# Layer norm of a feed-forward block: the two feature halves are added on VectorE, so that mean and variance are one TensorE product each

## What is computed

```python
x = x + o @ wo
h = shift_token(x)
mu = h.mean(-1, keepdims=True)
var = h.var(-1, keepdims=True)
h = (h - mu) / jnp.sqrt(var + 1e-05) * lg + lb
h = h @ w1 + b1
a, g = jnp.split(h, 2, axis=-1)
h = a * jax.nn.gelu(g, approximate=False)
x = x + h @ w2 + b2
```

## Time and profile before

| | |
|---|---|
| time, median of 3 runs | 2325.43 us (2323.35 to 2335.47) |
| profiled execution, its own time | 2311.7 us |
| span of the profiled execution | 2309.9 us |
| instructions | 28766 |
| PE busy | 2076.8 us, 90% of the span |
| DVE busy | 1063.5 us, 46% |
| ACT busy | 883.8 us, 38% |
| POOL busy | 684.8 us, 30% |
| mean granted TensorE clock | 0.964 |

### The profile page before, as it was taken

One profiled execution on the slowest core, in us unless ns is written; L12 is line 12 of the kernel. 1 busy time (PEld: TensorE's weight loads), 2 busy tenths in 40 slices (PEclk: granted clock), 3 DMA queues, 4 the chain that ended last, 5 costly groups with the idle time before them and its releaser, 6 DMA issues.

```text
span 2309.9 us, 28766 instructions
## 1 busy us (share of the span) xinstructions
PE 2076.8 (90%) x8914; PEld 1222.2 (53%) x8963; DVE 1063.5 (46%) x2012; ACT 883.8 (38%) x2175; POOL 684.8 (30%) x664
## 2 busy tenths in 40 slices
PE   4774999994899999998999999999999998999897
PEld 2532666662555555555555555555555555555553
DVE  5553222221554554553545535354555444554541
ACT  0021333331444445353534344344535353544432
POOL 6073000003532342342323416132252432232310
PEclk9976999997899999999999999999999999999999
DMA  8332221212100010100000001000010200000000
GB/s 248 124 126 96 62 59 59 61 57 55 28 10 1 1 28 1 37 19 29 1 1 10 19 28 28 19 11 1 1 28 1 44 12 19 1 0 1 1 13 15
DMA packets 71768, 78.19 MB, mean 34 GB/s; under 512 B 17156, under 2 KB 63704, under 8 KB 71640
## 3 DMA queue, kind: packets, MB, share of 16 engines
q1 hardware_dynamic: 56104, 58.68, 8.1%
q0 software_dynamic: 12672, 17.87, 3.9%
q10 hardware_dynamic: 2864, 0.01, 0.1%
HBM read 48.19 MB, written 28.35 MB: 33 GB/s over the span
## 4 chain that ended last, share of the span: by engine, by line
PE 52%; issue 8%; DVE 7%; ACT 5%; POOL 4%; DMA 1%; ACTq 0%; POOLq 0%; DVEq 0%
PE pj L1343 12%; PE pj L1252 10%; PE pj L1349 6%; PE ob L1303 6%; PE pj L1317 4%; PE sc L1279 4%; PE pt L1290 3%; DVE swapped L1528 3%; PE pj L1260 2%; POOL x1tok L1475 2%; ACT prob L1409 2%; PE sc L1272 1%; PE pj L1330 1%; PE pj L1242 1%; PE pj L1324 1%
## 5 line engine op out<-in xcount | busy, mean ns | idle before, releaser
L1486 POOL TENSOR_TENSOR qksq<-qkraw 128x512 f32<-128x512 f32 x128 | 162.7, 1296 | 871.1 <-ACT qkraw L1384 870.9
L1252 PE MATMUL pj<-wqkv,xT 128*128 128x512 f32 x768 | 348.4, 604 | 10.2 <-issue 10.2
L1343 PE MATMUL pj<-h,w 128*128 128x512 f32 (+1 forms) x704 | 338.6, 606 | 7.6 <-DVE h L1569 5.7
L1409 ACT ACTIVATE prob<-sc,nm 128x256 f32<-128x256 f32 (+1 forms) x512 | 222.0, 445 | 228.2 <-DVE nm L1543 225.9
L1303 PEld LDWEIGHTS ob<-vv,pT 128*128 128x128 f32 x1792 | 226.2, 195 | 77.3 <-issue 63.7
L1528 DVE TENSOR_TENSOR swapped<-qkraw,tabs 128x256 f32<-128x256 f32 x256 | 254.0, 1031 | 0.0
L1303 PE MATMUL ob<-vv,pT 128*128 128x64 f32 x1792 | 229.0, 275 | 23.7 <-DVE pT L1173 23.7
L1252 PEld LDWEIGHTS pj<-wqkv,xT 128*128 128x128 f32 x768 | 144.0, 193 | 191.5 <-issue 191.1
L1492 POOL TENSOR_TENSOR direct<-direct,swapped 128x512 f32<-128x512 f32 x128 | 187.5, 1480 | 73.3 <-DVE swapped L1528 73.3
L1523 DVE TENSOR_TENSOR direct<-qkraw,tabs 128x512 f32<-128x512 f32 x128 | 102.9, 804 | 203.1 <-ACT qkraw L1384 203.1
L1343 PEld LDWEIGHTS pj<-h,w 128*128 128x128 f32 (+1 forms) x704 | 120.9, 188 | 123.0 <-issue 115.4
(11 more groups left out here) (246 smaller groups left out, 2645.9 us busy)
## 6 DMA issues: line engine op xcount, KB each, us to landing
xt<-slots_x SPq DMA_DIRECT2D x72, 128.5 KB, 2.1
slots_y<-yt SPq DMA_DIRECT2D x72, 128.0 KB, 1.7
xin<-in_x_dram SPq DMA_DIRECT2D x8, 512.0 KB, 4.8
w1m<-in_L_ffn_w_dram SPq DMA_DIRECT2D x8, 512.0 KB, 10.5
w2m<-in_L_ffn_w_dram SPq DMA_DIRECT2D x8, 512.0 KB, 9.9
x1tok<-in_x_dram SPq DMA_DIRECT2D x8, 512.0 KB, 4.8
x_after_moe<-x1tok SPq DMA_DIRECT2D x8, 512.0 KB, 2.6
x1out<-x_after_moe SPq DMA_DIRECT2D x8, 512.0 KB, 4.5
```

Of the source, the lines that this page charges most:

```text
L1252: mm = pe.matmul(o[:, :], xs(s, c, w * P, P), wqkv[:, l, c, k * INNER:(k + 1) * INNER], start=(c == 0), stop=(c == DC - 1))
L1343: mm = pe.matmul(o[0:P if j == NJ - 1 else HJ[j], :], cols, h[:, c, :], start=(c == 0), stop=(c == DC - 1))
L1409: ins = a.activation(prob[:, g % 4, hh, 0:n], sc[par][:, hh, 0:n], ACT.Exp, bias=nm[:, g % 4, hh:hh + 1], accum_out=rs[:, st["win"] % 2, h ...
L1486: pool.tensor_tensor(qksq[:, k * INNER:(k + 1) * INNER], src, src, ALU.mult).then_inc(squared, 1)
```

## The change

Ahead of the mean product, DVE adds the two (shifted) halves of `xT` into `xsq[:, 0, :]`; PE then does one product over that sum instead of two over the halves. After the squares, DVE adds the two halves of `xsq` in place, and PE again does one product instead of two. Two semaphores, `xsum_ready` and `var_in`, hand the sums to PE. DVE's first addition is issued at the end of the step `wo` with c = 1, behind a wait for its own two additions into `xT`; the second is issued in the step `var`, where DVE had nothing before, behind a wait for ACT's squares.

```diff
                         elif kind == "mean":
-                            wait_taken(pe, st["wo_use"], i)
+                            pe.wait_ge(xsum_ready, at(st["ffn"], i, FFN, 1, 1))
                             o = bank(u, i)
-                            for c in range(DC):
-                                mm = pe.matmul(o[:, :], mean_w[:, :], xs(s, c), start=(c == 0), stop=(c == DC - 1))
-                            mm.then_inc(proj_full, 1)
+                            pe.matmul(o[:, :], mean_w[:, :], xsq[:, 0, :], start=True, stop=True).then_inc(proj_full, 1)
                         elif kind == "var":
-                            pe.wait_ge(xsq_ready, at(st["ffn"], i, FFN, 1, 1))
+                            pe.wait_ge(var_in, at(st["ffn"], i, FFN, 1, 1))
                             o = bank(u, i)
-                            for c in range(DC):
-                                mm = pe.matmul(o[:, :], mean_w[:, :], xsq[:, c, :], start=(c == 0), stop=(c == DC - 1))
-                            mm.then_inc(proj_full, 1)
+                            pe.matmul(o[:, :], mean_w[:, :], xsq[:, 0, :], start=True, stop=True).then_inc(proj_full, 1)
...
                             v.tensor_tensor(x_, o[:, :], x_, ALU.add).then_inc(proj_taken[u % NP], 1)
+                            if st["c"] == DC - 1:
+                                wait_taken(v, u - 1, i)
+                                wait_taken(v, u, i)
+                                v.tensor_tensor(xsq[:, 0, :], xs(s, 0), xs(s, 1), ALU.add).then_inc(xsum_ready, 1)
...
+                        elif kind == "var":
+                            v.wait_ge(xsq_ready, at(st["ffn"], i, FFN, 1, 1))
+                            v.tensor_tensor(xsq[:, 0, :], xsq[:, 0, :], xsq[:, 1, :], ALU.add).then_inc(var_in, 1)
```

More of the change, by code:

```diff
@@ L1127, in build @@
             xsq_ready = sem("xsq_ready")
+            xsum_ready = sem("xsum_ready")
+            var_in = sem("var_in")
             rstd_ready = sem("rstd_ready")
```

## The result

The changed kernel took 2358.12 us at the median of 4 runs (2355.45 to 2362.09), the kernel before 2324.39 us beside it. The ratio is 1.0146, 95% interval 1.0108 to 1.0183: slower by 1.5%, where no difference was forecast. In a second session it was 1.0107 (1.0075 to 1.0139). (A session is a set of runs made together on one chip; the kernel before was run in each.)

What follows compares the result with a forecast made beforehand. PE was taken to bound the kernel, with new links nearly cancelling 27.5 us of removed products: -2.5 - 2.4 + 3.1 + 0.4 = -1.4 us, plus 3 for the clock, from 2325.4 to 2327 us, range 2319 to 2334.

Steps and rivals of the forecast that it cites:

- The list and what bounds the kernel: PE, busy 90% of the span, bounds the kernel; 32 products of 0.86 us go, 32 DVE additions come.
- about 28 us less PE busy time: Sign expected in the profile after, from removing two products per layer norm, 27.5 us of PE work.
- Patterns A and B: A: nine layer norms (body blocks one and two, three in the tail), -2.5 us; B: three in block three, -2.4 us.
- The new link: Each DVE addition put ahead of a PE product: 0.68 us plus a 0.04 us hop, 0.72 us.
- patterns A, B and D: The 13 layer norms outside the body's fourth block; D, the tail's third, was put at +0.4 us.
- Pattern C, the first addition: Fourth block of the body, three layer norms: PE's wait for roped covers the addition and the mean's saving, net 0.
- Pattern C, the second addition: Fourth block, variance: the addition stands behind rr and on; 1.90 us standstill less 0.86, +1.04 three times, +3.1 us.
- The clock: Standstills in patterns C and D, four places: a shorter fall of PE's clock at two of them, +3 us.
- The second, the clock: Rival: the longer clock fall at all four late second additions, 13 us, 2337 us, 0.5% slower; chance 0.14.
- The price of the additions: Rival: additions cost 1.56 us each instead of 0.68 in patterns A and B, +21 us, 2347 us; chance 0.06.

Runs made afterwards that it cites:

- e3: The changed kernel with the fourth block of the body (three of 16 layer norms) left in the old form: 1.0017 of the kernel before.
- e5: The changed kernel, but the fourth block's first addition reads one operand from PSUM and skips its wait: 1.0040, again 1.0044, of the kernel before.
- e2: Only the variance product takes its sum from VectorE, the mean stays two products: 2341.47 us, 1.0069 of the kernel before.
- e4: The changed kernel with products of constants on PE ahead of its waits for VectorE's sums: 2330.94 us, 1.0021 of the kernel before.
- e1: Only the mean product takes its sum from VectorE, the variance stays two products: 2347.38 us, 1.0086 of the kernel before.
- e6: The kernel before plus the fourth block's first addition, for which only VectorE's own list waits; PE's products unchanged: 1.0032 of the kernel before.

## Why the prediction was wrong, point by point

**The list and what bounds the kernel: right.** PE bounds it, and of 27.5 us of product time removed none came through. The additions appear where they were forecast, and VectorE's busy time rose by 32.5 us (22 forecast; the 10.5 between are mostly time held). The sign "about 28 us less PE busy time" did not come: it is 8.0 us more.

**Patterns A and B: right in kind.** The new link was priced 0.72 and is 0.80 (0.69 + a hop of 0.10 to 0.11 us). For the 13 layer norms of patterns A, B and D the sum was -4.5 us, -0.2%. The ledger of e3 has -3.4 us for them. In the time nothing of a gain was found: +0.17% (-0.08 to +0.42) in e3 and +0.11% with fillers. So the sum was near, and what it left out, the clock, was as large as the gain.

**Pattern C, the first addition: the first step that failed.** I wrote that the wait for roped "covers a dearer first addition: even at 1.56 us PE comes to the transposes in time", and took 1.56 as the price beside GpSimd, though GpSimd's instructions stand one behind the other here and the earlier trace rows already gave 2.85 as the worst of 128. What came instead: 4.11, 4.12 and 4.78 us of standstill ahead of the mean product in the three rounds, 13.0 us where I had put nothing. With the wait for roped (3.5) that they cover, pattern C is +9.2 us by the ledger and not +3.1.

The rows of before bear a reckoning in place of a price: the addition ends 0.55 us after the GpSimd instructions that it has to wait out. In the row of 1.56 that is one (GpSimd 2175.33 + 1.04 = 2176.37 by the timeline, end 2176.92), in the row of 2.85 two, and in the 4.06 of after the rest of a run of four. How many it is went, in the rows looked at, with how close they stand. Two places of before:

```profile
602.68 2.31 POOL L1486 TENSOR_TENSOR qksq<-qkraw 128x512 f32<-128x512 f32 x2
602.71 2.85 DVE L1523 TENSOR_TENSOR direct<-qkraw,tabs 128x512 f32<-128x512 f32 x1 [1.95 <-ACT qkraw L1384]
...
625.14 2.48 POOL L1486 TENSOR_TENSOR qksq<-qkraw 128x512 f32<-128x512 f32 x2 [4.40 <-ACT qkraw L1384]
625.16 1.56 DVE L1523 TENSOR_TENSOR direct<-qkraw,tabs 128x512 f32<-128x512 f32 x1 [1.95 <-ACT qkraw L1384]
```

At 602 us GpSimd's second instruction began 0.22 us before the first had ended, and VectorE waited out both (end 605.56, GpSimd 604.99). At 625 us it began 0.04 us after the end of the first; there VectorE came in between, 0.54 us after the first, and GpSimd's second took 1.40 us instead of 1.04. In the fourth block the four stand like the first pair, each begun 0.6 us before the end of the one before it. Before the change GpSimd's run at this place ended at 991.47 + 2.63 = 994.10, by the timeline; by that reckoning the mean product, which started at 990.56, would have been put at 994.7, four microseconds late. The Trainium skill (SBUF — State Buffer, section on the two separate sides) says just this: VectorE with two SBUF inputs and a GpSimd instruction that reads SBUF share a pair of ports under an exclusive lock, and the loser waits out the whole instruction. The trace agrees, with e5's 0.68 us for one operand in PSUM beside it, and goes further: VectorE was held not for one instruction but to the end of the run, 4.06 us (three of the four, as it began in the second). I had looked for a price of the addition alone, not for who else was at work at its place.

**Pattern C, the second addition: right.** 1.90 us of standstill were forecast, 1.62 came in each round; e2 has the same 1.62 without the first addition.

**The clock: the second step that failed, and the larger one.** The mechanism was named, its size wrong by far: I put it at 3 us, and at 13 us in the rival with a chance of 0.14. The ledger puts 35.8 - 27.5 = 8.3 us on standstills, 4.8 without the wait for roped; the measured loss is 25 us in one session (1.07% of 2312) and 34 us in the other. So some 20 to 29 us are the clock's, and e4 gives back 20 to 29; by PE's busy time in the profiled execution it is 37. I counted only the four longest new standstills, with a fall at two of them. But 16 layer norms got two each, and those of 0.3 to 3.3 us cost clock too, with no held addition among them: e5 has a clock of 0.955 against 0.961, e3 0.955 against 0.959, and in the changed kernel the tail is at 0.96 against 0.98 before. Not each one does: the block at 785 to 796 us ran at full clock through standstills of 0.74 and 1.88 us. Which do, I can't say from the rows.

**The rivals.** The second, the clock (2337, slower), named the right mechanism and the right way, but tied it to four places and left out the held addition, and 2358 lies far beyond it. The price of the additions as a rival was put everywhere, at 1.56, instead of in one place, at 4 us; and against it I had said that POOL is idle at the places of patterns A and B, which does not hold for the third block, whose three additions took 0.90 us.

**Open.** e1 and e2 add up to 1.55%, the whole change in two sessions 1.46% and 1.07%, with intervals that overlap; whether the sessions differ in it is not settled. The two profiles of the changed kernel say where such a difference would lie: the standstills at the two products are the same (21.9 and 26.0 us, 21.8 and 26.0), while from the first layer norm to the end PE is busy for 1552.1 us in one and 1535.7 in the other, at a clock of 0.96 and 0.97. What sets the clock apart in two executions of one kernel the runs do not show. That no gain was left in the 13 layer norms with fillers is measured, not explained.

## What to carry to other kernels

Before a VectorE instruction with both inputs in SBUF is put on the path, look in the timeline at what GpSimd does at that place: here it was held until GpSimd's whole run of instructions was over, and one operand in PSUM freed it. To take work from a PE that is 90% busy and put a wait in its stead was no gain here, even where the wait was as short as the work: the standstill cost its length, and the many of them cost clock as well. Products of constants in the standstills showed in one run that most of the loss was the clock.

## What the runs showed of the hardware that I had not expected

- A 128x512 float32 addition with two SBUF operands took 4.05 to 4.73 us where it met a run of four GpSimd products, and 0.68 us with one operand in PSUM at the same place. GpSimd's own pairs were not slowed there: 3.10 and 2.63 us before, 3.08 and 2.61 after, and in e6 3.09 and 2.62. Where GpSimd began its next instruction 0.04 us after the end of the last, VectorE came in between, and GpSimd's took 1.40 us instead of 1.04.
- 39 us of useless products on the bounding engine made the changed kernel 20 to 29 us faster, and its granted clock went from 0.946 and 0.953 to 0.959.
- The same kernel before took 2312 us in two sessions and 2324 to 2329 in three others, while its ratios to its variants held (e5: 1.0040 and 1.0044); only ratios of one session are worth comparing here.
